# Stablemax attention of the fourth layer: half of the heads keep their two terms apart until TensorE multiplies them with V

## The reference

```python
def stablemax(x):
    s = jnp.where(x >= 0, x + 1.0, 1.0 / (1.0 - x))
    return s / jnp.sum(s, axis=-1, keepdims=True)
...                                  # q, k, v: 16 heads of 8 features, keys and values from ctx
scores = jnp.einsum('bhqd,bhkd->bhqk', q, k) / np.sqrt(HD).astype(np.float32)
attn = stablemax(scores)
context = jnp.einsum('bhqk,bhkd->bhqd', attn, v)
context = context.transpose(0, 2, 1, 3).reshape(b, -1, E)
return context @ Wo.T + bo
```

## Time and profile before

| | |
|---|---|
| median of 3 runs | 2562.04 us (2560.22 to 2562.13) |
| the profiled execution | 2556.09 us, span of its instructions 2554.3 us |
| PE, DVE, ACT, POOL busy over the span | 85%, 71%, 53%, 48% |
| mean granted TensorE clock over the span | 0.902 of full speed |
| fourth attention, first to last join (L1057) | 2061.2 to 2371.8 us of the span |
| its experts | from about 2384 us to the end |

### The profile page before, as it was taken

The page is one execution under the profiler, slowest core; times in us unless marked ns, Lnnn a source line. Parts: engine busy times, 40 slices in busy tenths (PEclk is TensorE's granted clock), DMA queues, the critical chain, the costliest instruction groups (busy, mean ns, idle before and its releaser), DMA issues. The chain is left out here.

```text
span 2554.3 us, 78270 instructions
## 1 busy us (share of the span) xinstructions
PE 2168.7 (85%) x32243; PEld 1663.2 (65%) x32243; DVE 1823.6 (71%) x5057; ACT 1356.6 (53%) x2507; POOL 1213.6 (48%) x1728
## 2 busy tenths in 40 slices
PE   6999999999987959997555999993999688787597
PEld 5887887878864747775443677772566457666375
DVE  4777777777773658888985688986455388999454
ACT  3555555555542338787995555550222177788232
POOL 1334434344344531116773145556566666887444
PEclk9999999999998979998876999995999866888599
DMA  6320000000006621110000011112555322332363
GB/s 199 112 110 27 27 24 27 22 22 20 19 18 182 174 63 54 58 50 7 1 1 20 27 45 54 52 44 79 155 160 161 91 79 60 98 94 71 94 187 102
DMA packets 213955, 184.50 MB, mean 72 GB/s; under 512 B 33420, under 2 KB 189654, under 8 KB 213600
## 3 DMA queue, kind: packets, MB, share of 16 engines
q1 hardware_dynamic: 194144, 142.52, 19.2%
q0 software_dynamic: 19456, 36.99, 4.2%
HBM read 102.01 MB, written 72.68 MB: 68 GB/s over the span
## 5 line engine op out<-in xcount | busy, mean ns | idle before, releaser
L614 POOL DMA_INDIRECT slots<-row,put x256 | 258.6, 1010 | 193.1 <-issue 129.7
L1941 PE MATMUL experts_H<-experts_xs_t,experts_w 128*128 128x512 f32 x576 | 265.6, 605 | 6.9 <-DMA experts_b<-in_F_b 2.6
L1097 ACT ACTIVATE l_prob_t<-l_banks 128x512 f32<-128x512 f32 x256 | 132.2, 602 | 146.1 <-PE l_banks L1214 116.5
L1467 POOL TENSOR_TENSOR l_var_eps<-l_mv,eps 128x1 f32<-128x1 f32 x64 | 12.2, 191 | 413.9 <-DVE l_mv L1548 413.9
L1959 PE MATMUL experts_Y<-experts_w,experts_hid 128*128 128x128 f32 x1664 | 197.8, 275 | 3.5 <-DVE experts_y L1889 2.6
L1806 POOL DMA_INDIRECT rows<-experts_y,experts_idx x160 | 155.5, 972 | 91.4 <-DVE experts_y L1885 50.9
L1959 PEld LDWEIGHTS experts_Y<-experts_w,experts_hid 128*128 128x128 f32 x1664 | 191.7, 192 | 5.4 <-issue 5.4
L1503 DVE TENSOR_REDUCE l_top<-l_S 128x16 f32<-128x1024 f32 x64 | 78.3, 1224 | 160.4 <-PE l_S L1646 160.4
L1941 PEld LDWEIGHTS experts_H<-experts_xs_t,experts_w 128*128 128x128 f32 x576 | 106.1, 194 | 115.9 <-issue 107.2
L1008 DVE TENSOR_REDUCE l_top<-l_banks 128x32 f32<-128x2048 f32 x64 | 146.5, 2289 | 48.0 <-PE l_banks L1221 36.3
L912 POOL TENSOR_TENSOR l_var_eps<-l_mv,eps 128x2 f32<-128x2 f32 x96 | 24.1, 251 | 307.7 <-DVE l_mv L978 216.5
(11 more groups left out here) (312 smaller groups left out, 6041.3 us busy)
## 6 DMA issues: line engine op xcount, KB each, us to landing
experts_w<-in_F_w SPq DMA_DIRECT2D x104, 256.0 KB, 3.6
l_ctx_t<-in_ctx_t SPq DMA_DIRECT2D x96, 128.0 KB, 2.4
early_q_m<-l_q_t SPq DMA_DIRECT2D x384, 32.0 KB, 1.8
experts_xs<-slots SPq DMA_DIRECT2D x40, 264.0 KB, 2.9
slots<-l_empty SPq DMA_DIRECT2D x16, 536.0 KB, 4.0
experts_xs<-slots SPq DMA_DIRECT2D x16, 536.0 KB, 4.4
slots<-l_empty SPq DMA_DIRECT2D x16, 520.0 KB, 6.0
experts_xs<-slots SPq DMA_DIRECT2D x16, 520.0 KB, 4.4
```

Of the source, the lines that this page charges most:

```text
L614: pool.indirect_dma_start(self.slots, bass.IndirectOffsetOnAxis(ap=g.put[c][:, tile:tile + 1], axis=0), g.row[:, tile, self.sent_cols], No ...
L1097: nc.scalar.activation(prob_t[:, t.par(PROB), r, :], Z[:, r, :], ACT.Exp).then_inc(prob_done, 1)
L1941: nc.tensor.matmul(H[:, c, :], w1_s[:, t.par(2), c, :], xs_t[:, t.par(2), :], start=True, stop=True).then_inc(h_filled[c], 1)
```

## The change

The join covers the first two of the four groups of heads only (`JOINED = 2`), 1024 columns in place of 2048. For heads 8 to 15 `soft` holds only the second term and `prob_t` the first. TensorE multiplies both with the same `val` slice and adds in PSUM: heads 0 to 7 take 16 products as before, heads 8 to 15 take 32 in place of 16. Per item that is 48 products (96 passes) in place of 32 (64 passes). The semaphores and waits are the same, TensorE still waits for `joined` ahead of all products, and nothing else moves. The forms for the second and third attention are as before. Lines behind the insertions stand one to four numbers lower in the file (L1057 becomes L1058, L1271 becomes L1274).

```diff
@@ attention_split @@
     SLOTS_QK, SLOTS_CTX = 4, 8
+    JOINED = 2
     LAST = STREAM + 1
@@ block.vector, step @@
                     wait(dve, plus_done, 4 * t.done(PROB))
                     wait(dve, prob_done, t.done(PROB))
-                    V.tensor_tensor(soft[:, t.par(PROB), :, :], soft[:, t.par(PROB), :, :], prob_t[:, t.par(PROB), :, :], ALU.add).then_inc(joined, 1)
+                    V.tensor_tensor(soft[:, t.par(PROB), 0:JOINED, :], soft[:, t.par(PROB), 0:JOINED, :], prob_t[:, t.par(PROB), 0:JOINED, :],
+                                    ALU.add).then_inc(joined, 1)
@@ block.tensor, step @@
-                    term = soft if stable else prob_t
                     for h in range(16):
+                        terms = [prob_t] if not stable else [soft] if h // 4 < JOINED else [soft, prob_t]
                         for tile in range(2):
                             col = 256 * tile + 64 * (h % 4)
-                            last = nc.tensor.matmul(O[64 * tile:64 * tile + 64, 18 * h:18 * h + 18], term[:, t.par(OUT), h // 4, col:col + 64],
-                                                    val[:, t.par(OUT), tile, h, :, :].rearrange("p b c -> p (b c)"), start=True, stop=True)
+                            for term in terms:
+                                last = nc.tensor.matmul(O[64 * tile:64 * tile + 64, 18 * h:18 * h + 18], term[:, t.par(OUT), h // 4, col:col + 64],
+                                                        val[:, t.par(OUT), tile, h, :, :].rearrange("p b c -> p (b c)"),
+                                                        start=term is terms[0], stop=term is terms[-1])
                     last.then_inc(o_filled, 1)
```

## The result

The changed kernel takes 2529.76 us (median of 4 runs, 2526.46 to 2542.76) against 2562.09 before; the ratio is 0.9891, 95% interval 0.9862 to 0.9919, which is 28 us of 2562. The profiled execution took 2529.54 us, 26.6 less than that of before.

The account below looks back on a forecast made before the run. The prediction took a loop of join, GpSimd and VectorE's statistics as the bound, with TensorE's clock deciding. 252 + 14.4 + 4.8 = 271.2 us against 284.2 gains 13, less 3 at the end: 2552 us, range 2533 to 2573.

Parts of the forecast that it names:

- The circle of join, GpSimd and statistics: Fourth attention: the join holds GpSimd, whose combination VectorE's statistics await before the next join; 9.51 us a step becomes 8.39.
- TensorE's circle: Fourth attention, TensorE from turning one result through the products to the next turn; 6.83 us becomes 7.85 at full clock.
- The price of the products: TensorE's 32 more passes per item: 2.05 us becomes 3.07 at full clock, 3.61 becomes 5.42 at low; PSUM adding free.
- ScalarE is near: ScalarE's work of 8.15 us per item lies 0.24 below the new 8.39 us step, so it is late next.
- the low clock through the products in 3 of 28 steps: Fourth attention: three steps of 13.8 us in place of 9.0, 4.8 us each, adding 14.4 us.
- a late L1254 in 6: TensorE's L1254 ends late in six of 28 steps of the fourth attention, adding 0.8 us each, 4.8 us.
- the rival: The clock stays at 2.4 GHz through the fourth attention; 28 steps near 9.0 us, about 2533 us in all; 15%.
- The count of falls: Falls of TensorE's granted clock within 28 items of the fourth attention: 8 instead of 12.
- The forecast clock: TensorE's granted clock from the first to the 29th join: above 0.79, about 0.85.
- The step from the profiled execution to the median: Whole kernel: the profiled 2556.09 us lies 5.95 below the median 2562.04; the gain was applied to the median.
- The even exchange at the old clock: Fourth attention with the clock as before: gains and losses sum to +0.2 us; as a rival 2562 within 5, 20%.
- The last four items: End of the fourth attention, two of the items at the low clock before: a loss of about 3 us.

Follow-up runs that it names:

- half join alone: The changed kernel without the added products, so heads 8 to 15 leave out a part of the numerator; 2526.18 us, 0.9883 of the kernel before.
- The repeat: The changed kernel itself, unaltered, measured a second time; 2529.35 us, 0.9902 of the kernel before.
- the products alone: The kernel before, all four groups still joined, with the products of heads 8 to 15 done twice; 2573.88 us, 1.0069 of the kernel before.

## Why the prediction was right in its direction and small in its size

- The circle of join, GpSimd and statistics: right. The join takes 1.22 us (1.16 said), undisturbed steps 8.45 (8.39), steps with a batch 9.9 and 9.25, on average 9.0 as said. The half join alone shows that it carries the gain. TensorE's circle is less in the way than the prediction's signs had it: VectorE's reciprocal waits for the products in 8 of 28 steps, not in most.
- The price of the products: right. 3.00 us at the full clock (3.07), 5.32 to 5.34 at the low one (5.42), and adding in PSUM costs nothing that can be seen.
- ScalarE is near: right. It idles 14.4 + 10.4 = 24.8 us before L1097 and L1134 (about 30 said).
- The term that was mis-sized is "the low clock through the products in 3 of 28 steps", 14.4 us set against the gain. It was nothing in the profiled execution: of the 28 items only the first had its products partly at the low clock. The other term, "a late L1254 in 6", 4.8 us, came out as said, 4 to 5 us more than 8.45, 9.9 and 9.25 in the steps that a fall touched, but shorter steps at the start made up for most of it. So 28 items took 253.4 us where the forecast had 271.2 and the rival 254.
- The count of falls was off too. The prediction has 12 in the 28 items of before and forecasts 8. The granted clock falls there 14 times, and four of the low stretches last 17.1 us; in the changed kernel it falls 8 times, each for 3.4 us only. So the number 8 is partly luck, and what decided was the length. The forecast clock of 0.85 became 0.94.
- The size of the error depends on the execution. The repeat has two steps with the products at the low clock, and 28 items in 262.8 us, half way to the forecast. Three was too many for these two executions; the mechanism, and its price of some 4 us a step, is there.
- The step from the profiled execution to the median added 5.95 us to the forecast. In the changed kernel the two are 0.2 us apart, so about 6 us of the 22 between 2552 and the median come from there. By the median the result lies 3 us below the lower end of the range, 2533; by the ratio it is 2534.
- The even exchange at the old clock was not tested, since every run with a shorter join has a higher clock. Of its parts the products alone, at 0.84, lost 8.6 us of stage. That the same products are nearly free behind the short join goes with the gap that the two together leave, 0.73 us per item in place of 1.40, but that is argued and not shown apart. The prediction is also at odds with itself here: by its own sum four steps at the low clock would leave a gain of 5 us, not none.
- The last four items lost 2 us in this execution (28.6 us from the 29th join to the last, 26.5 before; 3 said), at a clock of 0.62. The repeat took 21.7, so that this agreement is luck.
- The price of the Trainium skill ("TensorE: Matmul & The Clock Gate", LDWEIGHTS) for a stationary load, 53 ns for 64 columns, does not hold at the full clock here: 96 passes in 3.00 us are 31 ns each. The rule of the Trainium skill ("TensorE: Matmul & The Clock Gate", Why this matters for your kernels) that continuous work keeps the clock up and idle gaps between bursts lower it was the better guide to the size. The clocks and gaps of the thirteen traces agree with it: 0.79 at 1.40 us per item, 1.00 at 0.19.

What stays open: why the clock comes back after 3.4 us in one place and after 17.1 in another. The traces show what hangs on it. In the stages of all kernels here each low stretch of 13.7 or 17.1 us that begins in the first 28 items holds one whole set of products, which starts 5 or 8 us into it, and no shorter one does. So a fall is cheap if the clock is back before the products. What decides whether it is, no run tried apart.

## What to carry to other kernels

When a change gives work from VectorE to TensorE in a loop where TensorE idles between thin products, price the stage at both clocks, and read from the trace what TensorE did before each fall: the same added passes cost 8.6 us of stage here behind the long join and 2.6 or 5.1 behind the short one. The wide VectorE add of two SBUF tensors held GpSimd's small instructions while it ran (3.03 us for a power that takes 0.72 alone), so look for GpSimd instructions that are slow only beside it, and count the VectorE instruction on GpSimd's path too. Once the bound moves, try the neighbouring settings: one group joined was 13 us better than two.

## What the runs showed of the hardware that was not expected

Useless dense work made a kernel faster: 16 passes per item in the gap, 1.95 us, took the clock from 0.79 to 0.96 and 0.30% (0.17 to 0.44) off the time. And the code ahead of the stage, the same in all kernels, ends at different times from one execution to the next: the first join started between 2057.9 and 2069.3 us of the span in the profiles, so a difference of less than some 10 us between two single executions says nothing unless it is read inside the stage. Inside it one and the same kernel differed by 9.4 us over 28 items, about 8 of them in the two steps with the products at the low clock.
